# An AdaLN block with an H3 attention and a mixture of experts: spectral units spread over two batch rows, the barrier ahead of the heads left out, and three smaller reorderings

## The chip, the cores and the metric

The kernel runs on one core of a Trainium2 chip. The metric is the device time of one execution in microseconds (us); the times shown are those of the runs named below. Engines: TensorE (PE in the rows; PEld its weight load), VectorE (DVE), ScalarE (ACT), GpSimd (POOL) and SyncE (SP), which issues most DMAs.

## The reference

Four batch rows of 1024 tokens with 256 features, 32 bit. Two modulated layer norms enclose an H3 attention and a top-2 mixture of eight experts:

```python
mod = (silu(c) @ wmod).reshape(4, 6, 1, 256)
sa, ca, ga, sb, cb, gb = ...
h = layernorm(x) * (1 + ca) + sa
x = x + ga * h3_attention(h)
h = layernorm(x) * (1 + cb) + sb
x = x + gb * moe(h)

def h3_attention(u):
    q, k, v = (u @ W.T + b for each of three)
    k = causal_conv(k, ssm_k_kernel) + ssm_k_D * k
    kv = k[:, :, i] * v[:, :, j]
    y = causal_conv(kv, ssm_kernel) + D * kv
    return (q * y).sum(over i) @ Wo.T + bo
```

Heads are groups of 8 features (32 of them), so each head convolves 64 products. The taps are 512 long in both convolutions. The experts take at most 1280 tokens each.

## The kernel before

Everything lives in SBUF: `qkv` holds q, v and k of all 32 tiles of 128 tokens, and a large `arena` is cut into regions by hand, so who may write where is a matter of order. Each engine has its own program, written out in order, and waits on semaphores; there is no scheduler.

**Rows.** For each batch row `b`, TensorE turns the normalised row (`h_transposes`, L1325), VectorE modulates the turned pieces (`h_rows`, L860, four a row), ScalarE and GpSimd split them into a high and a low part, and TensorE makes eight tiles of q, v and k (`qkv_products`, L1344), twelve matmuls each. Two pairs of PSUM banks take the tiles in turn, and tile t waits until VectorE has added the bias to tile t - 2 (`qkv_rows`, L900).

**Units.** The convolution of k goes through a spectrum. A unit is half the columns of one batch row, eight in all. For each unit TensorE runs `forward` (L1365, 16 matmuls of 256 columns, f32), ScalarE copies four banks (`spec_out`, L683), VectorE joins the parities, turns a half, multiplies by the spectrum of the taps and folds (`joined_spectrum` to `folded_product`, L368 to L415), TensorE runs `inverse` (L1379), and ScalarE copies the result into `k_stage` (`conv_out`, L691). There are two buffers of spectra and two of folded products. `forward(0)` stands after the third row, `forward(1)` in the middle of the fourth, and after that inverses alternate with forwards three ahead. VectorE makes units 0 and 1 between the bias adds of the fourth row, beginning after the third.

**Turning K.** From `k_stage` SyncE sends k back into the token layout in `qkv`, one batch row (two units) at a time, four DMAs of 256 KB each (L473 to L478). Both engines that reuse `k_stage` or read k wait for `k_turned`.

**Barrier.** After this stage every engine drains and waits for all five (`stage_end`, L337). SyncE loads the first two Toeplitz blocks of the heads just ahead of it:

```python
            sp.wait_ge(fold_ready[1], UNITS)
            load_toeplitz(0)
            load_toeplitz(1)
            sp.wait_ge(k_turned, 64 * (B + 1))
            stage_end(sp, 1)
```

**Heads.** For each of 32 heads VectorE multiplies k and v (`products`, L1001, four quarters), ScalarE and GpSimd split products and Toeplitz block (L705 on, L569 to L578), TensorE multiplies (L1436), and VectorE gates and sums.

**Behind the heads.** For each row: `y_transposes`, `attention_out`, then `residual` and statistics on VectorE, `normalize` on ScalarE (L725, eight tiles, one signal), `h2_transposes` (L1468, four groups in two banks), copies with the modulation (`h2_turned`, L734), `router` (L1481), logits and choice on VectorE. After that come a threshold search and the experts.

At the start TensorE runs five matmuls on zeros (L1288), the modulation, the first transposes, and then waits for the split of the first row.

## Time and profile before

| | us |
|---|---|
| median of 3 runs | 1224.91 (1223.55 to 1226.75) |
| profiled execution, its own time | 1222.99 |
| span of its profile | 1221.2 |
| TensorE busy | 1123.6 (92% of the span) |
| VectorE busy | 820.2 (67%) |
| ScalarE busy | 420.5 (34%) |
| GpSimd busy | 546.0 (45%) |

The profile is of one execution; its span begins and ends a little inside the time that is measured. Times in the rows are microseconds from the start of the span. Of the chain of work that ended last, the page puts 83% on TensorE, 7% on VectorE and 2% each on ScalarE, DMA, GpSimd and time without a visible wait. A busy share says little by itself here: the stages have different limits, so the stretch around the change has to be read by itself. By stretches, the rows of the batch and the units lie from 17 to 233 us, the heads from 244 to about 580, the routing to about 660, and the rest is the threshold search and the experts.

### The profile page before, as it was taken

Reading aid. Unit: us, or ns where it says so; the run is one execution under the profiler, and the core shown is the slowest. Engines: PE = TensorE matmul, PEld = TensorE weight load, DVE = VectorE, ACT = ScalarE, POOL = GpSimd, SP = SyncE. Lnnn points to the kernel's source line nnn. Section 1 sums busy time; section 2 is a strip of 40 time slices with the busy share of each in tenths; the row PEclk is TensorE's granted clock in tenths of the full one; section 3 lists DMA queues with packets and bytes.
Section 4 is the critical chain, followed back from the end, with each engine's and each line's share of the span. In section 5 each row is a group of like instructions: output and inputs, shape, how many; then the busy total and the mean of one; then the engine's idle time right before and its main releaser. Section 6 shows DMA issues by size and latency. Waiting matters only on the chain.

```text
span 1221.2 us, 16986 instructions
## 1 busy us (share of the span) xinstructions
PE 1123.6 (92%) x5754; PEld 974.4 (80%) x5754; DVE 820.2 (67%) x1549; ACT 420.5 (34%) x762; POOL 546.0 (45%) x403
## 2 busy tenths in 40 slices
PE   7999999499999999999985548999999999999996
PEld 5878888388888888887775447889898989899996
DVE  5576999579999999999576785454444444444442
ACT  5321222223333333331562212343443534344432
POOL 3130000177777777774000022566565656565723
PEclk8999999799999999999985557999999999999998
DMA  7100022343111011002440212754544443534322
GB/s 263 35 35 1 1 52 50 104 142 102 32 32 32 32 32 32 32 21 69 139 144 7 100 56 68 192 146 68 134 91 117 83 121 79 132 73 78 60 42 27
DMA packets 69633, 93.35 MB, mean 76 GB/s; under 512 B 5668, under 2 KB 57636, under 8 KB 69592
## 3 DMA queue, kind: packets, MB, share of 16 engines
q1 hardware_dynamic: 51576, 60.96, 15.9%
q0 software_dynamic: 18016, 31.86, 13.6%
q8 instruction: 24, 0.39, 0.1%
q14 instruction: 17, 0.14, 0.0%
HBM read 65.29 MB, written 23.31 MB: 73 GB/s over the span
## 4 chain that ended last, share of the span: by engine, by line
PE 83%; DVE 7%; issue 2%; ACT 2%; DMA 2%; POOL 2%; SPq 0%; DVEq 0%; POOLq 0%; ACTq 0%
PE ps L1436 27%; PE ps L1575 18%; PE ps L1591 12%; PE ps L1592 6%; PE ps L1386 5%; PE ps L1375 4%; PE ps L1356 4%; PE ps L1464 2%; DVE arena L1141 1%; PE ps L1557 1%; PE ps L1485 1%; DVE qkv L819 1%; DMA qkv<-in_w 1%; PE ps L1537 1%; DVE arena_rounded L819 1%
## 5 line engine op out<-in xcount | busy, mean ns | idle before, releaser
L1575 PE MATMUL ps<-arena_rounded,w_high 128*128 128x384 f32 (+1 forms) x768 | 211.4, 356 | 2.1 <-DVE arena_rounded L819 2.1
L578 POOL TENSOR_TENSOR kv_low<-arena,kv_high 128x512 fp32r<-128x512 f32 x128 | 187.1, 1491 | 38.7 <-ACT kv_high L630 38.7
L1436 PE MATMUL ps<-kv_high,toep_high 128*128 128x512 f32 (+1 forms) x512 | 193.9, 379 | 11.1 <-POOL kv_low L578 11.1
L1436 PE MATMUL ps<-kv_low,toep_high 128*128 128x512 f32 (+1 forms) x512 | 193.9, 379 | 0.0
L1436 PE MATMUL ps<-kv_high,toep_low 128*128 128x512 f32 (+1 forms) x512 | 193.0, 377 | 0.0
L1258 DVE SCALAR_TENSOR_TENSOR hidden_low<-ps,hidden_high 128x384 fp32r<-128x384 f32 (+1 forms) x192 | 115.6, 602 | 100.1 <-ACT hidden_high L788 99.7
L602 POOL DMA_INDIRECT out<-arena x80 | 126.2, 1578 | 105.1 <-DVE arena L819 97.4
L591 POOL DMA_INDIRECT qkv<-row_scratch,arena x80 | 82.6, 1033 | 185.3 <-DVE arena L1212 159.2
L1575 PEld LDWEIGHTS ps<-arena_rounded,w_high 128*128 128x128 f32 x768 | 140.4, 190 | 13.4 <-issue 2.5
L819 DVE TENSOR_TENSOR arena<-qkv 128x512 f32 (+1 forms) x128 | 136.8, 1127 | 12.5 <-SPq L339 12.5
L788 ACT ACTIVATE hidden_high<-ps 128x384 fp32r<-128x384 f32 (+1 forms) x192 | 101.3, 528 | 126.7 <-PE ps L1575 126.7
L573 POOL TENSOR_TENSOR toep_low<-arena,toep_high 128x640 fp32r<-128x640 f32 x32 | 50.1, 1566 | 198.4 <-ACT toep_high L630 198.4
L1575 PE MATMUL ps<-arena_rounded,w_low 128*128 128x384 f32 (+1 forms) x384 | 136.5, 355 | 0.0
L1268 DVE SCALAR_TENSOR_TENSOR arena<-ps,qkv,arena 128x256 f32<-128x256 f32 x80 | 38.7, 484 | 139.1 <-ACT arena L803 139.1
L1436 PEld LDWEIGHTS ps<-kv_high,toep_high 128*128 128x128 f32 x512 | 96.9, 189 | 29.9 <-POOL kv_low L578 11.5
L1591 PE MATMUL ps<-arena_rounded,hidden_high 128*128 128x512 f32 x320 | 113.1, 397 | 3.2 <-DVE arena L1268 3.2
L1591 PE MATMUL ps<-qkv_rounded,hidden_high 128*128 128x512 f32 x320 | 113.6, 398 | 0.0
L630 ACT ACTIVATE kv_high<-arena 128x512 fp32r<-128x512 f32 x128 | 78.7, 632 | 100.1 <-DVE arena L819 100.1
L1436 PEld LDWEIGHTS ps<-kv_high,toep_low 128*128 128x128 f32 x512 | 96.7, 189 | 18.0
L1436 PEld LDWEIGHTS ps<-kv_low,toep_high 128*128 128x128 f32 x512 | 97.0, 189 | 17.7
L1019 DVE TENSOR_REDUCE qkv<-arena 128x512 f32 (+1 forms) x128 | 87.8, 686 | 18.9 <-DVE arena L819 4.7
L819 DVE TENSOR_TENSOR arena<-ps,qkv 128x512 f32<-128x512 f32 x128 | 87.4, 683 | 13.5 <-PE ps L1436 13.4
(194 smaller groups left out, 1954.2 us busy)
## 6 DMA issues: line engine op xcount, KB each, us to landing
arena<-ssm_scratch SPq DMA_DIRECT2D x32, 320.0 KB, 3.2
qkv<-in_w SPq DMA_DIRECT2D x16, 512.0 KB, 5.1
qkv<-in_w SPq DMA_DIRECT2D x8, 1024.0 KB, 8.8
arena<-in_u SPq DMA_DIRECT2D x7, 1024.0 KB, 6.2
row_scratch<-qkv SPq DMA_DIRECT2D x4, 1056.0 KB, 4.6
qkv<-arena SPq DMA_DIRECT2D x16, 256.0 KB, 3.4
row_scratch<-arena SPq DMA_DIRECT2D x4, 1024.0 KB, 6.4
out<-qkv SPq DMA_DIRECT2D x4, 1024.0 KB, 9.3
```

The costliest lines, as they stand in the source:

```text
L578: nc.gpsimd.tensor_tensor(kv_parts[s][1][:, quarter], kv_flat[s][:, quarter], kv_parts[s][0][:, quarter].bitcast(F32), ALU.subtract).then_ ...
L591: nc.gpsimd.indirect_dma_start(qkv[:, 16 + j, D:WIDE], None, row_dram[:, :], bass.IndirectOffsetOnAxis(ap=from_row[:, column:column + 1], ...
L602: nc.gpsimd.indirect_dma_start(out[:, :], bass.IndirectOffsetOnAxis(ap=to_row[:, column:column + 1], axis=0), y_sb[column % RING], None, c ...
L630: return nc.scalar.activation(dst, src, ACT.Copy)
L788: nc.scalar.activation(hid_parts[0][:, BANK * f:BANK * f + width], ps[:, f % 4, 0:width], ACT.Relu).then_inc(hid_high, 1)
L819: return nc.vector.tensor_tensor(o, a, b_, op)
L1019: nc.vector.tensor_reduce(qkv[:, tiles, bass.ds(h * NJ, NJ)], qy[g], AX.X, ALU.add).then_inc(head_summed, 1)
L1258: nc.vector.scalar_tensor_tensor(hid_parts[1][:, BANK * f:BANK * f + width], ps[:, f % 4, 0:width], 0.0, hid_parts[0][:, BANK * f:BANK * f ...
L1436: last = mm(ps[:, 4 * s + g, (lo - 2 * g) * B * 64:BANK], toep_parts[s][a][:, o * P:(o + 1) * P], kv_parts[s][x][:, src], start=n == 0 and ...
L1575: last = mm(ps[:, f % 4, 0:width], w1_parts[q][a][:, dc * F + f * P:dc * F + (f + 1) * P], xeT_parts[x][dc][:, 0:width], start=dc == 0 and ...
L1591: mm(ps[:, bank].rearrange("p (a d) -> p a d", a=2), high, w2_parts[q][:, :, f], start=f == 0, stop=False)
L1592: last = mm(ps[:, bank, 0:D], low, w2_parts[q][:, 0, f], start=False, stop=f == FC - 1)
```

## The change

- **Units.** `forward(0)` moves into the third row, after its sixth tile, `forward(1)` behind that row's last tile, `forward(2)` into the middle of the fourth row and `forward(3)` behind it; inverses then alternate with forwards four ahead. VectorE joins unit 0 ahead of the third row's last bias add, makes the rest of unit 0 before the fourth row's adds, and units 1 and 2 between them, four adds each. The second `clamp` of the modulation moves from tile 6 to tile 3 of the third row.
- **Buffers.** There are three folded buffers (unit 1 has a place of its own), and unit 0 has its own spectrum buffer.
- **Turning K.** SyncE turns K by unit, with DMAs of 128 KB (rows of 512 bytes), one semaphore for each parity of the unit.
- **Barrier.** It is left out. The Toeplitz block of head 0 is loaded ahead of the first turn, that of head 1 after unit 2, both to other places. VectorE makes the products of heads 0 and 1 by batch row, three rows as soon as they are turned, the last when its two units are.
- **Filler.** Four matmuls of 512 columns follow the first transposes; 24 matmuls of 128 columns follow the last inverse.
- **Router.** `normalize` signals after four tiles and after eight; transposes go by half row, and the router starts on a half.

The core of the diff; buffer addresses and declarations are left out:

```diff
+FILL_FIRST, FILL_HEADS = 4, 24
...
+        def spectrum_of(unit):
+            return parity_spec[0 if unit == 0 else 1 + unit % 2]
+        def folded_of(unit, parity):
+            return (folded_1 if unit == 1 else folded[unit % 3])[parity]
...
         def folded_product(dve, link, unit):
-            if unit >= 2:
-                dve.wait_ge(conv_psum, CT * (unit - 1))
+            if unit >= 3:
+                dve.wait_ge(conv_psum, CT * (unit - 2))
...
-            with sp.Fori(0, B) as b:
-                for parity in range(2):
-                    sp.wait_ge(conv_ready, 2 * CT * b + 2 * CT + (parity + 1) * CT // 2)
-                    for half in range(2):
-                        dst = tile_view[parity::2, half::2, bass.ds(b, 1), 2 * D:3 * D].rearrange("p t o n -> p t (o n)")
-                        sp.dma_start(dst, k_stage[half * P // 2:(half + 1) * P // 2, parity::2]).then_inc(k_turned, 16)
...
-            sp.wait_ge(fold_ready[1], UNITS)
             load_toeplitz(0)
-            load_toeplitz(1)
-            sp.wait_ge(k_turned, 64 * (B + 1))
-            stage_end(sp, 1)
+            for unit in range(UNITS):
+                e = slice(2 * D + columns(unit).start, 2 * D + columns(unit).stop)
+                for parity in range(2):
+                    sp.wait_ge(conv_ready, CT * unit + CT + (parity + 1) * CT // 2)
+                    for half in range(2):
+                        sp.dma_start(tile_view[parity::2, half::2, unit // 2, e],
+                                     k_stage[half * P // 2:(half + 1) * P // 2, parity::2, columns(unit)]).then_inc(k_turned[unit % 2], 16)
+                if unit == 2:
+                    load_toeplitz(1)
+            for i in range(2):
+                sp.wait_ge(k_turned[i], 64 * B)
...
-                    if i == 0 and unit % 2 == 0:
-                        act.wait_ge(k_turned, 32 * unit + 64)
+                    if i == 0 and unit >= 2:
+                        act.wait_ge(k_turned[unit % 2], 64 * (unit // 2))
...
-                last.then_inc(norm2_ready, 1)
+                    last.then_inc(norm2_ready, 1)
...
-                    if b == 2 and t == 6:
+                    if b == 2 and t == 3:
                         clamp(GB - 2)
+                    if b == 2 and t == TB - 1:
+                        dve.wait_ge(consts_in, 16 * 8)
+                        joined_spectrum(dve, link, 0)
...
+            for unit, t in ((1, 0), (2, TB // 2)):
+                qkv_rows(B - 1, t)
+                joined_spectrum(dve, link, unit)
+                qkv_rows(B - 1, t + 1)
+                turned_half(link)
+                qkv_rows(B - 1, t + 2)
+                real_products(link, unit)
+                qkv_rows(B - 1, t + 3)
...
-            stage_end(dve, 1)
...
-            products(0, 0)
-            products(1, 1)
+            for b in range(B - 1):
+                for i in range(2):
+                    dve.wait_ge(k_turned[i], 64 * (b + 1))
+                for h in range(2):
+                    first_products(h, b)
+            for i in range(2):
+                dve.wait_ge(k_turned[i], 64 * B)
+            for h in range(2):
+                first_products(h, B - 1).then_inc(kv_ready, 4)
...
+            for _ in range(FILL_FIRST):
+                mm(ps[:, 7, :], idle[:, 0:P], idle, start=True, stop=True)
...
+                if b == B - 2:
+                    qkv_products(b, range(TB // 2, TB - 2))
+                    forward(0)
+                    qkv_products(b, range(TB - 2, TB))
+                    forward(1)
+                    continue
                 if b == B - 1:
-                    forward(1)
+                    forward(2)
                 qkv_products(b, range(TB // 2, TB))
...
-                if b == B - 2:
-                    forward(0)
-            forward(2)
+            forward(3)
...
                 inverse(unit)
-                if unit + 3 < UNITS:
-                    forward(unit + 3)
-            stage_end(pe, 1)
+                if unit + 4 < UNITS:
+                    forward(unit + 4)
+            pe.wait_ge(spec_ready, JP * UNITS + 4)
+            pe.wait_ge(consts_in, 16 * 8)
+            for _ in range(FILL_HEADS):
+                mm(ps[:, 0, 0:P], group_ones[:], ident[:], start=True, stop=True)
...
                 for g in range(4):
+                    half, dc = g // 2, g % 2
+                    if dc == 0:
+                        pe.wait_ge(norm2_ready, 2 * b + half + 1)
...
-                pe.wait_ge(h2T_ready, 4 * b + 4)
                 for tb in range(TB):
+                    if tb % 4 == 0:
+                        pe.wait_ge(h2T_ready, 4 * b + tb // 2 + 2)
```

VectorE, from the end of the third row, before. The line L819 on 128x768 is a bias add, L363 and L364 the join, L377 and L378 the turned half, L387 and L388 the real products:

```order
L819 TENSOR_TENSOR qkv<-ps,arena 128x768 x3
L363 TENSOR_TENSOR arena<-arena 128x512
L364 TENSOR_TENSOR arena<-arena 128x512
L363 TENSOR_TENSOR arena<-arena 128x512
L364 TENSOR_TENSOR arena<-arena 128x512
L819 TENSOR_TENSOR qkv<-ps,arena 128x768
L377 SCALAR_TENSOR_TENSOR arena<-arena,sign_sb 128x4x128
L378 SCALAR_TENSOR_TENSOR arena<-arena,sign_sb 128x4x128
L819 TENSOR_TENSOR qkv<-ps,arena 128x768
L387 TENSOR_TENSOR arena<-arena 128x1024
```

The same place of the change; its lines are L821 for the add, L368 and L369 for the join, L382 and L383 for the turned half, L392 to L407 for products, difference and sum, L418 for the fold:

```order
L368 TENSOR_TENSOR arena<-arena 128x512
L369 TENSOR_TENSOR arena<-arena 128x512
L821 TENSOR_TENSOR qkv<-ps,arena 128x768
L382 SCALAR_TENSOR_TENSOR arena<-arena,sign_sb 128x4x128
L383 SCALAR_TENSOR_TENSOR arena<-arena,sign_sb 128x4x128
L392 TENSOR_TENSOR arena<-arena 128x1024
L393 TENSOR_TENSOR arena<-arena 128x1024
L397 TENSOR_TENSOR arena<-arena 128x1024
L402 TENSOR_TENSOR arena<-arena 128x1024
L403 TENSOR_TENSOR arena<-arena 128x1024
L407 TENSOR_TENSOR arena<-arena 128x1024
L418 TENSOR_TENSOR arena<-arena 128x512 x4
```

Before, an add of the fourth row stands between every two steps of unit 0. In the change the add in this piece is the third row's last, and the rest of unit 0 runs to its fold without an add.

TensorE, from the last forwards to the first head, before. L1375 is a forward, L1386 an inverse, L1436 a head:

```order
L1375 MATMUL ps<-qkv,arena 128x256 x16
L1386 MATMUL ps<-arena 128x256 x16
L1375 MATMUL ps<-qkv,arena 128x256 x16
L1386 MATMUL ps<-arena 128x256 x48
L1420 UNCONDITIONAL_BRANCH
L1420 ISA
L1425 ISA
L1436 MATMUL ps<-kv_high,toep_high 128x512
```

And in the change, where L1391 is a forward, L1402 an inverse, L1440 the filler and L1459 a head:

```order
L1391 MATMUL ps<-qkv,arena 128x256 x16
L1402 MATMUL ps<-arena 128x256 x16
L1391 MATMUL ps<-qkv,arena 128x256 x16
L1402 MATMUL ps<-arena 128x256 x64
L1440 MATMUL ps<-ident_sb,group_ones_sb 128x128 x24
L1443 UNCONDITIONAL_BRANCH
L1443 ISA
L1448 ISA
L1459 MATMUL ps<-kv_high,toep_high 128x512
```

Four inverses, not three, stand behind the last forward, and 24 filler matmuls behind them.

## Rows read from the trace of the kernel before

**Rows 1.** Chain of work in order of time: start us, us, what

```profile
74.34 8.58 PE ps L1356 x48
...
133.90 6.91 PE ps L1386 x32
...
216.81 7.15 issue
223.96 8.99 PE ps L1386 x32
232.98 0.39 ACT arena L630
...
234.22 3.52 DMA qkv<-arena
...
242.26 1.73 POOL kv_low L578
```

**Rows 2.** Windows: stretch, us, each engine's busy time, granted TensorE clock, DMA share, GB/s

```profile
17.00:22.80 5.80, 5.80 (x21) 5.22 (x22) 2.88 (x7) 0.68 (x2) 0.46 (x1) 0.50 0.90 306
216.90:220.80 3.90, 0.00 (x0) 0.00 (x0) 3.83 (x4) 0.33 (x1) 0.00 (x0) 1.00 0.00 0
221.00:227.60 6.60, 3.64 (x9) 2.95 (x10) 4.03 (x6) 0.00 (x0) 0.00 (x0) 0.50 0.00 0
244.00:248.00 4.00, 3.98 (x11) 3.30 (x12) 3.59 (x4) 1.26 (x2) 4.00 (x3) 0.50 0.83 328
```

**Rows 3.** Timeline of VectorE: start us, us, engine, line, operation, tiles, count

```profile
88.03 0.81 DVE L867 TENSOR_SCALAR arena<-ps,modT 128x512 f32<-128x512 f32 x1 [0.44 <-POOL hT_low L561]
...
90.49 0.53 DVE L873 TENSOR_SCALAR arena<-arena 4x256 f32<-4x256 f32 x1
...
92.67 0.96 DVE L819 TENSOR_TENSOR qkv<-ps,arena 128x768 f32<-128x768 f32 x1
...
121.50 1.82 DVE L819 TENSOR_TENSOR qkv<-ps,arena 128x768 f32<-128x768 f32 x2 [0.15 <-DVE arena L413]
...
139.26 0.69 DVE L363 TENSOR_TENSOR arena<-arena 128x512 f32<-128x512 f32 x1 [0.15 <-DVE arena L413]
...
141.91 0.75 DVE L377 SCALAR_TENSOR_TENSOR arena<-arena,sign_sb 128x512 f32<-128x512 f32 x1
...
211.11 0.69 DVE L363 TENSOR_TENSOR arena<-arena 128x512 f32<-128x512 f32 x1 [0.15 <-DVE arena L413]
...
237.80 8.42 DVE L819 TENSOR_TENSOR arena<-qkv 128x512 f32<-128x512 f32 x8 [12.55 <-SPq L339]
```

**Rows 4.** Page, costliest groups: ScalarE's split of products, busy and mean ns, idle before

```profile
L630 ACT ACTIVATE kv_high<-arena 128x512 fp32r<-128x512 f32 x128 | 78.7, 632 | 100.1 <-DVE arena L819 100.1
```

**Rows 5.** Source view of L478, the sixteen DMAs that turn K

```profile
DMA to landing us min/median/max: 3.2/3.4/3.6
```

**Rows 6.** Timeline of TensorE at the start

```profile
1.47 6.70 PE L1288 MATMUL ps<-arena 128*128 128x512 f32 x10 [1.47 <-DVE arena L930]
...
16.92 0.76 PE L1356 MATMUL ps<-wqkv_high,hT_high 128*128 128x512 f32 x1 [4.70 <-POOL hT_low L561]
...
22.45 0.67 PE L1356 MATMUL ps<-wqkv_high,hT_high 128*128 128x512 f32 x1
```

**Rows 7.** Timeline of all engines, router of the first and the last row

```profile
596.49 1.10 PE L1477 MATMUL ps<-ident_sb,qkv 128*128 128x128 f32 x8 [0.52 <-ACT qkv L730]
...
637.85 4.04 ACT L730 ACTIVATE qkv<-qkv,shift,std 128x256 f32<-128x256 f32 x8 [0.47 <-DVE shift L1060]
...
641.94 3.95 PE L1477 MATMUL ps<-ident_sb,qkv 128*128 128x128 f32 x16 [2.37 <-ACT qkv L730]
...
645.08 1.63 ACT L738 ACTIVATE arena<-ps,modT 128x512 f32<-128x512 f32 x2 [0.35 <-PE ps L1477]
...
646.76 6.99 PE L1485 MATMUL ps<-wr_sb,arena 128*128 128x8 f32 x32 [0.87 <-ACT arena L738]
...
653.79 0.23 DVE L1073 COPY arena<-ps 128x64 f32<-128x64 f32 x1 [0.86 <-PE ps L1485]
```

More of the change, by code:

```diff
@@ L185, in adaln_block @@
         kv_parts = [parts(f"kv{i}", FT + 4096 * i, [P, 2048]) for i in range(2)]
-        toep_raw = [region(WQ0 + TOEP * i, TOEP) for i in range(2)]
+        toep_raw = [region(start, TOEP) for start in (KK0 + 3328, MA0 + 2 * TOEP)]
         toep_parts = [parts(f"toep{i}", start, [P, TOEP]) for i, start in enumerate((KK0, MA0))]
@@ L269, in adaln_block @@
         row_dram = nc.dram_tensor("row_scratch", [TOKENS, ROW], F32)
-        stage_done = [sem(f"stage{k}_done") for k in range(8)]
         chain_v, chain_g = sem("vector_chain"), sem("gpsimd_chain")
@@ L412, in folded_product @@
                     j = part * JP // 2
-                    last = nc.vector.tensor_tensor(folded[unit % 2][parity][:, j:j + JP // 2], v[:, 0:JP // 2], v[:, JP // 2:JP], op)
+                    last = nc.vector.tensor_tensor(folded_of(unit, parity)[:, j:j + JP // 2], v[:, 0:JP // 2], v[:, JP // 2:JP], op)
                 link(last)
@@ L687, in spec_out @@
                     act.wait_ge(spec_psum, JP * unit + j + 1)
-                    copy(parity_spec[unit % 2][:, 2 * j:2 * j + 2],
+                    copy(spectrum_of(unit)[:, 2 * j:2 * j + 2],
                          ps[:, j].rearrange("p (o h e) -> p o h e", o=2, h=2)).then_inc(spec_ready, 1)
@@ L693, in conv_out @@
                     act.wait_ge(conv_psum, CT * unit + i + 1)
-                    if i == 0 and unit % 2 == 0:
-                        act.wait_ge(k_turned, 32 * unit + 64)
+                    if i == 0 and unit >= 2:
+                        act.wait_ge(k_turned[unit % 2], 64 * (unit // 2))
                     copy(k_stage[:, c::CT, columns(unit)],
                          ps[:, 4 + c, 0:D].rearrange("p (h e) -> p h e", h=2)).then_inc(conv_ready, 1)
-            for unit in range(3):
+            for unit in range(4):
                 spec_out(unit)
@@ L702, in _ @@
                 conv_out(unit)
[L703 to L705 removed]
+                if unit + 4 < UNITS:
+                    spec_out(unit + 4)
             with act.Fori(0, HEADS // 2) as hh:
@@ L978, in _ @@
             folded_product(dve, link, 0)
-            qkv_rows(B - 1, 4)
-            qkv_rows(B - 1, 5)
-            joined_spectrum(dve, link, 1)
-            qkv_rows(B - 1, 6)
-            turned_half(link)
-            qkv_rows(B - 1, 7)
-            real_products(link, 1)
-            real_difference(link)
-            imaginary_products(link, 1)
-            imaginary_sum(link)
-            folded_product(dve, link, 1)
-            for unit in range(2, UNITS):
+            for unit, t in ((1, 0), (2, TB // 2)):
[6 more added lines that the diff above has]
+                qkv_rows(B - 1, t + 3)
+                real_difference(link)
+                imaginary_products(link, unit)
+                imaginary_sum(link)
+                if unit == 1:
+                    dve.wait_ge(hT_low, 4 * B)
+                    dve.wait_ge(mod_out, 16)
+                folded_product(dve, link, unit)
+            for unit in range(3, UNITS):
                 joined_spectrum(dve, link, unit)
@@ L1386, in inverse @@
                         last = mm(ps[:, 4 + c, 0:D].rearrange("p (h e) -> p h e", h=2), idft[:, j, c * P:(c + 1) * P],
-                                  folded[unit % 2][c % 2][:, j], start=j == 0, stop=j == JP - 1)
+                                  folded_of(unit, c % 2)[:, j], start=j == 0, stop=j == JP - 1)
                     last.then_inc(conv_psum, 1)
```

50 lines of the change are left out of this document (21 added, 29 removed).

## The prediction

> **What bounds the kernel now.** I read the page's chain first: TensorE carries most of it, so what counts is where TensorE waits or runs at its low clock. The chain in order of time then shows one large hole around the change [rows 1]. The seventh inverse ends at 216.81, TensorE stands 7.15 us until VectorE has folded unit 7, the last inverse takes 8.99 instead of 6.91 us, and from its end at 232.95 another 11.1 us pass before the first head multiplies at 244.0: a copy, a DMA of 3.52 us, products, splitting on ScalarE and GpSimd. The table of windows gives the clock beside it [rows 2]: 1.2 GHz (0.50) from 221.0 to 227.6 and again for the first 4 us of the heads; earlier also from 17.0 to 22.8, after an idle of 4.70 us [rows 6]. In the idle of 7.15 us the clock was still up after 4.0 us and down by 4.2. VectorE's timeline [rows 3] says why the hole exists: five units take 71.85 us from 139.26 to 211.11, 14.37 each, while TensorE needs 2 x 6.91 = 13.82 a unit, so VectorE is behind when the last unit comes.
>
> **1. Units inside the third and fourth rows.** VectorE's work stays the same and starts sooner, but its bias adds, which free TensorE's banks, now stand behind unit work. I walk both queues with: a tile 8.58/4 = 2.15 us, a forward or inverse 6.91 [rows 1]; a bias add 0.86 to the next instruction and 0.96 to its end, a join 141.91 - 139.26 = 2.65, the other steps of a unit 11.72 [rows 3].
> The second clamp, 92.67 - 90.49 = 2.18 us, moves ahead of the last row's four transposed pieces. The last of these started at 88.03 and took 0.81 [rows 3]; now it ends at 91.0. Forward 0 needs it. TensorE's first four tiles of row three end at 82.92 [rows 1], its transposes and two more tiles at 88.9, so it idles 2.2 us. Forward 0 runs to 98.0, tiles 6 and 7 to 102.3, forward 1 to 109.2, tiles 0 and 1 of the last row to 113.5. VectorE meanwhile: add 6 at 100.2, join 0 to 103.7, add 7 to 104.6, rest of unit 0 to 116.3, add 0 done at 117.3. Tile 2 waits for that add: **idle 3.8 us**. Tile 3 waits for the next add, behind join 1, until 120.8 (1.3 us); forward 2 ends at 129.9, tiles 4 and 5 at 134.2. Unit 1 with its four adds ends at 116.3 + 14.37 + 3.4 = 134.1, so tile 6 starts at 135.1 (0.9 us) and tile 7 at 138.6 (1.4 us). Forward 3 ends at 147.7; twelve forwards and inverses without a gap follow, 82.9 us, to 230.6. VectorE ends unit 2 at 152.0 and five more at 223.8; the last inverse begins at 223.7 and needs only the first of the fold's two halves. So TensorE becomes the bound, with about 1 us to spare: the 7.15 us and the low clock of the last inverse go, and 9.6 us of smaller idles take their place. Against 232.95 that is 2.3 us; the restarts after five idles are not in the walk, so I take **2.0** (0.5 to 2.5). With the third folded buffer each inverse that VectorE asks for has ended over 8 us before.
>
> **2. The gap ahead of the heads.** The barrier itself cost nothing: the DMA landed at 237.74 and VectorE started at 237.80 [rows 1, 3]. What shrinks is the work. From the end of the last inverse: copy 0.42, two DMA issues 0.85, landing, one product 8.42/8 = 1.05 [rows 3], ScalarE's split 0.63 [rows 4], GpSimd's 1.73 [rows 1], 0.2 of handovers. The Toeplitz block, which GpSimd split first, is now loaded early and split while the DMA flies. Three quarters of the products are made beside the last inverse (six of 1.05 us after 223.8, done at 230.1). For the landing of half the bytes the nearest row is the sixteen DMAs of now, 3.2 to 3.6 us [rows 5]; below that nothing in the rows excludes 2.3. I take 3.2, since the smaller size was never seen. Sum 8.1 against 11.1: **3.0** (2.6 to 3.9).
> The Trainium skill ("DMA: Bandwidth & Descriptors", Anatomy of one DMA) gives a fixed cost of about 2.0 us and the bytes over 436 GB/s; by that, an estimate, 128 KB land in 2.3 us and the gain would be 3.9. It is fitted for GpSimd's queue, and no run here shows this size.
>
> **3. Filler matmuls ahead of the heads.** 24 matmuls of 128 columns, f32. An inverse makes 32 records of 256 columns in 6.91 us, 0.216 each [rows 1]; 48 records of half the columns take 48 x 0.108 = 5.2 us. They stand in the 8.1 us gap and leave an idle of 2.9, less than the 4.0 after which the clock was still up [rows 2]. So the heads start at 2.4 GHz. Before, 4.0 us ran at half [rows 2], worth 2.0. At full clock the first quarter (2304 columns) takes 1.0 us and GpSimd's next split 1.73 [rows 1], so 0.7 comes back as a wait: **1.3** (0 to 2.0). From there the heads are one stretch of TensorE, so all of this reaches the end.
>
> **4. Filler at the start.** Four matmuls of 512 columns between 12.2 and 16.92. Five of the same took 6.70 us [rows 6], 1.34 each: 5.4 us, to 17.6, where the first tile is ready at 16.92. That tile and eight transposes took until 22.45 at 1.2 GHz, 5.5 us; at 2.4 GHz they take 2.15 + 0.9. The second tile then starts at 20.7 instead of 22.45, and its own first record was slow too (0.67). VectorE's add of that tile stands ahead of row two's statistics, and those ahead of the transposes that TensorE waits for next, so it is handed on: **2.0**. If the clock never falls, 2.6; if the filler is slow throughout (to 19.0) and the clock rises no sooner than now, a loss of 2.0.
>
> **5. Half-row router.** A row's first transposes need only four of eight scaled tiles. In the first row TensorE waited 0.52 us for the eighth [rows 7]; that and a copy brought forward give 0.6. In the last row ScalarE scales from 637.85 (4.04 us), TensorE waits until 641.94, the last copy ends at 646.71, and the router takes 6.99 at the low clock [rows 7]. Now the first two groups are turned from 639.9; groups three and four follow at 642.8 and 643.9, each once a copy (0.82) has freed its bank; the router starts on its first half at 644.9 and ends at 651.9 instead of 653.75. VectorE reaches that logit copy (653.79 now) at 652.0, since the exponential ahead of it comes 1 us sooner. 1.8 + 0.6 = **2.4** (1.0 to 3.0).
>
> **Sum.** 2.0 + 3.0 + 1.3 + 2.0 + 2.4 = 10.7 us. The profiled execution took 1222.99 us (span 1221.2): 1212.3. The median of the runs shown is 1.9 above it, so **1214.2**.
>
> **Rivals.**
> *The clock falls in the new idle of 3.8 us.* It held for 4.0 and was down by 4.2 [rows 2], so it is close. The price is that of the last inverse, 8.99 - 6.91 = 2.1 [rows 1], on a TensorE that is now the bound: 1216.3. Chance 0.17. The Trainium skill ("TensorE: Matmul & The Clock Gate", HAM oscillation) names just such gaps between matmuls as what throttles the engine again; by that rule this is the case that comes.
> *The filler at the start does nothing or costs.* It begins where the clock is about to fall. 2.0 to 4.0 lost: 1216.2 to 1218.2, say 1217. Chance 0.13.
> *Hardly any gain.* Both of these, and the heads begin at the low clock as well: 10.7 - 2.1 - 4.0 - 1.3 = 3.3, or 1221.6. Here the edits do not do what they say. Chance 0.06.
> *Slower: the clock stays low through the fourth row.* After the idle of 3.8 us come three of 0.9 to 1.4 within 25 us. If these keep it at 1.2 GHz until 140.8, six tiles and forward 2, 19.8 us of work, take twice as long; the idles absorb 3.6, and 16.2 goes through: 1230.4. It decides from about 18 us of such work on (10.7 + 3.7 + 3.6). Against it: after 7.15 us of idle the clock was back within 4 us of work [rows 1, 2]. Chance 0.03.
> *More than forecast.* Landing at 2.3, clock held at the start: 1212.7 or a little below. Chance 0.06.
>
> **How the numbers follow.** The forecast has 0.55. The range takes in the better case, the first two rivals and a little of their overlap: 1209.5 to 1219.5. Within 0.3% (3.7 us) is about what a measurement of this kernel cannot tell from no change; above 1221.2 lie only part of the third rival and the fourth. Faster 0.89, the same 0.07, slower 0.04.
>
> **What would show it.** No idle before the last inverse, which takes 6.9 us and ends near 228.6 (230.6 less the 2.0 of the start); idles of about 2 and 4 us in the third and fourth rows; a first head some 8 us after the last inverse, at 2.4 GHz from its first matmul; a last router that ends 2.4 us sooner after the heads. Wrong would be an idle before the last inverse (VectorE still bounds), or a granted clock of 0.50 behind the 3.8 us idle or at the first head.

## The result and the profile after

The changed kernel takes **1212.36 us**, median of four runs (1209.35 to 1213.68), beside 1225.83 for the kernel before in the same comparison: a ratio of 0.9888 with a 95% interval of 0.9876 to 0.9899, so 12.4 to 15.2 us less. One of the kernel before's four executions there took 1316.28 us, in a slower state of the chip; it is in that median (1224.91 without it) and not in the ratio. The profiled execution took 1209.35 us (span 1207.5), the lowest of the four; the one before took 1222.99. The span's 13.7 us, cut at five points that both traces have (TensorE's times):

| stretch | before | after | gain |
|---|---|---|---|
| start to the end of the last inverse | 232.94 | 228.79 | 4.15 |
| from there to the first head | 11.09 | 6.34 | 4.75 |
| first head to the first matmul behind the heads (`y_transposes`) | 330.97 | 329.29 | 1.68 |
| from there to the first matmul of the threshold search | 84.53 | 83.39 | 1.14 |
| from there to the end of the span | 561.67 | 559.69 | 1.98 |

In the tables below the third stretch is called the heads, the fourth the routers and the fifth the rest. The change does not touch the rest.

TensorE at the start, from the four filler matmuls on, two records each (they answer to [rows 6]). Columns are start, duration, engine, line, operation, tiles, shape, count, idle before and what ended it:

```profile
13.43 4.67 PE L1379 MATMUL ps<-arena 128*128 128x512 f32 x8
...
20.82 0.48 PE L1370 MATMUL ps<-wqkv_high,hT_high 128*128 128x512 f32 x1
```

The second tile starts 1.63 us sooner, although the weights of the modulation came 0.76 us later here (9.55 instead of 8.79 for the first matmul on them).

TensorE from the third row to the heads:

```profile
89.08 7.14 PE L1391 MATMUL ps<-qkv,arena 128*128 128x256 f32 x32 [1.97 <-issue]
...
115.38 0.80 PE L1370 MATMUL ps<-wqkv_high,hT_high 128*128 128x512 f32 x1 [3.87 <-DVE qkv L821]
...
136.63 0.50 PE L1370 MATMUL ps<-wqkv_high,hT_high 128*128 128x512 f32 x1 [0.85 <-DVE qkv L821]
...
213.73 15.06 PE L1402 MATMUL ps<-arena 128*128 128x256 f32 x69
228.62 5.52 PE L1440 MATMUL ps<-ident_sb,group_ones_sb 128*128 128x128 f32 x48
235.13 0.50 PE L1459 MATMUL ps<-kv_high,toep_high 128*128 128x512 f32 x1 [0.99 <-POOL kv_low L580]
```

Of the idle of 7.15 us and the slow last inverse [rows 1] nothing is left: the inverses run without a gap. In their place stand 1.97, 3.87 and 0.85 us. The windows answer to [rows 2] (granted clock third from the end):

```profile
115.40:122.00 6.60, 6.60 (x21) 5.55 (x22) 6.42 (x9) 0.00 (x0) 0.00 (x0) 0.55 0.00 0
129.20:135.70 6.50, 6.50 (x38) 5.59 (x36) 6.03 (x10) 0.60 (x1) 0.00 (x0) 1.00 0.00 0
235.00:241.00 6.00, 5.87 (x28) 4.84 (x29) 2.76 (x4) 3.00 (x6) 6.00 (x6) 1.00 0.86 303
```

The granted clock did fall at the end of the idle of 3.87 us (the window from 115.4 has 0.55), and the two tiles behind it ran at 1.2 GHz. It was back at 1.00 for the next tiles, and the heads start at 2.4 GHz. The gap ahead of the heads, on VectorE, ScalarE and GpSimd:

```profile
221.68 3.70 DVE L821 TENSOR_TENSOR arena<-qkv 128x512 f32<-128x512 f32 x6 [0.22 <-DVE arena L418]
232.38 1.29 DVE L821 TENSOR_TENSOR arena<-qkv 128x512 f32<-128x512 f32 x2 [6.99 <-DMA qkv<-arena]
...
228.82 0.38 ACT L632 ACTIVATE arena<-ps 128x256 f32<-128x256 f32 x1 [1.34 <-PE ps L1402]
...
233.10 2.19 ACT L632 ACTIVATE kv_high<-arena 128x512 fp32r<-128x512 f32 x4 [3.27 <-DVE arena L821]
...
229.91 1.54 POOL L575 TENSOR_TENSOR toep_low<-arena,toep_high 128x640 fp32r<-128x640 f32 x1 [138.92 <-ACT toep_high L632]
233.81 5.02 POOL L580 TENSOR_TENSOR kv_low<-arena,kv_high 128x512 fp32r<-128x512 f32 x4 [2.36 <-ACT kv_high L632]
```

GpSimd now splits the Toeplitz block while the DMA flies. In the kernel before, ScalarE could split that block only from 239.50 on, when its load had landed, 1.8 us behind K. And of the eight products of then [rows 3] the first five took 3.10 us and the last three, beside GpSimd's splits, 5.41:

```profile
239.50 0.74 ACT L630 ACTIVATE toep_high<-arena 128x640 fp32r<-128x640 f32 x1 [6.14 <-DMA arena<-ssm_scratch]
...
237.80 3.10 DVE L819 TENSOR_TENSOR arena<-qkv 128x512 f32<-128x512 f32 x5 [12.55 <-SPq L339]
240.81 5.41 DVE L819 TENSOR_TENSOR arena<-qkv 128x512 f32<-128x512 f32 x3
```

So a product by itself took 0.62 to 0.65 us in both kernels, and 1.05 was a mean of two kinds. GpSimd's four splits take 5.02 now, 1.26 each. The DMAs of half the size land faster than the old ones [rows 5]:

```profile
DMA to landing us min/median/max: 2.4/2.4/3.2
```

The last router, ScalarE, TensorE and VectorE (they answer to [rows 7]):

```profile
628.33 4.04 ACT L732 ACTIVATE qkv<-qkv,shift,std 128x256 f32<-128x256 f32 x8 [0.47 <-DVE shift L1074]
...
630.45 1.97 PE L1501 MATMUL ps<-ident_sb,qkv 128*128 128x128 f32 x8 [1.51 <-ACT qkv L732]
634.91 6.83 PE L1510 MATMUL ps<-wr_sb,arena 128*128 128x8 f32 x32
...
642.07 0.22 DVE L1087 COPY arena<-ps 128x64 f32<-128x64 f32 x1
```

From the first scaling to VectorE's copy of the logits it takes 13.74 us instead of 15.94.

### The profile page after: what moved, and what is told of

Read it like the earlier page. It is cut to its first block, busy times and chain, and to the rows that moved or that the text cites. A ratio compares the mean times of both kernels' runs of the same rounds, so it can differ in the third digit from the quotient of the medians.

```text
span 1207.5 us, 17088 instructions
## 1 busy us (share of the span) xinstructions
PE 1129.0 (93%) x5810; PEld 980.5 (81%) x5810; DVE 816.3 (68%) x1549; ACT 420.4 (35%) x762; POOL 544.8 (45%) x403
## 4 chain that ended last, share of the span: by engine, by line
PE 73%; issue 13%; DVE 7%; ACT 2%; DMA 2%; POOL 2%; SPq 0%; DVEq 0%; POOLq 0%; ACTq 0%
PE ps L1459 27%; PE ps L1600 18%; PE ps L1616 12%; PE ps L1617 6%; PE ps L1487 2%; PE ps L1370 2%; DVE arena L1155 1%; PE ps L1582 1%; DMA qkv<-in_w 1%; DVE qkv L821 1%; PE ps L1562 1%; DVE arena_rounded L821 1%; PE ps L1545 1%; PE ps L1510 1%; ACT qkv L732 1%
## 5 line engine op out<-in xcount | busy, mean ns | idle before, releaser
L1459 PE MATMUL ps<-kv_high,toep_high 128*128 128x512 f32 (+1 forms) x512 | 193.1, 377 | 1.0 <-POOL kv_low L580 1.0
L1459 PE MATMUL ps<-kv_low,toep_high 128*128 128x512 f32 (+1 forms) x512 | 193.1, 377 | 0.0
L1459 PE MATMUL ps<-kv_high,toep_low 128*128 128x512 f32 (+1 forms) x512 | 192.4, 376 | 0.0
L821 DVE TENSOR_TENSOR arena<-qkv 128x512 f32 (+1 forms) x128 | 133.3, 1099 | 7.2 <-DMA qkv<-arena 7.0
L1459 PEld LDWEIGHTS ps<-kv_high,toep_high 128*128 128x128 f32 x512 | 96.4, 188 | 19.7 <-POOL kv_low L580 1.2
L1459 PEld LDWEIGHTS ps<-kv_high,toep_low 128*128 128x128 f32 x512 | 96.1, 188 | 18.0
L1459 PEld LDWEIGHTS ps<-kv_low,toep_high 128*128 128x128 f32 x512 | 96.4, 188 | 17.4
L821 DVE TENSOR_TENSOR arena<-ps,qkv 128x512 f32<-128x512 f32 x128 | 87.4, 683 | 15.5 <-PE ps L1459 15.4
```

The costliest lines, as they stand in the source:

```text
L821: return nc.vector.tensor_tensor(o, a, b_, op)
L1459: last = mm(ps[:, 4 * s + g, (lo - 2 * g) * B * 64:BANK], toep_parts[s][a][:, o * P:(o + 1) * P], kv_parts[s][x][:, src], start=n == 0 and ...
```

## The experiments

Each is the changed kernel with one edit, or with one set of edits where the text says so. In the expectations "mine" is the author's account and "rival" another one. "Median" is that of its runs; the kernel before had medians of 1226.5 to 1227.5 beside them, so one comparison may lie about a microsecond off another. The columns after it are the stretches of the table above, from each one's profiled execution.

| run | median | end of last inverse | gap | heads | routers | rest |
|---|---|---|---|---|---|---|
| changed, again | 1211.33 | 229.36 | 6.40 | 329.30 | 83.37 | 559.9 |
| no filler at the start | 1212.80 | 232.17 | 6.41 | 329.29 | 83.38 | 560.2 |
| no filler ahead of the heads | 1215.17 | 228.82 | 6.36 | 330.45 | 85.03 | 562.6 |
| whole-row router | 1215.97 | 229.45 | 6.33 | 329.27 | 84.57 | 563.1 |
| barrier | 1217.28 | 229.98 | 9.46 | 330.65 | 83.66 | 560.3 |
| two folded buffers | 1219.29 | 235.39 | 6.34 | 329.29 | 83.60 | 563.2 |
| late clamps | 1209.63 | 226.94 | 6.35 | 329.29 | 83.39 | 562.5 |
| filler in the fourth row | 1214.15 | 230.18 | 6.35 | 329.31 | 83.38 | 563.6 |
| adds inside the units | 1214.38 | 231.45 | 6.36 | 329.27 | 83.38 | 562.3 |
| early forward | 1208.59 | 226.50 | 6.36 | 329.28 | 83.38 | 560.6 |
| the same, filler ahead of the last inverse | 1209.87 | 224.59 | 6.40 | 329.28 | 85.02 | 563.7 |
| the same, VectorE's order changed | 1214.40 | 228.44 | 7.53 | 330.88 | 83.41 | 562.4 |

The rest is the same program in all, and yet takes 560 to 564 us. Most of this goes with the clock. In the first group of experts TensorE waits 1.8 us for VectorE, and behind that wait the clock held in one execution (first fence: changed, again) and fell in another (second: late clamps). Windows, with the granted clock third from the end:

```profile
748.50:752.50 4.00, 2.31 (x13) 2.04 (x14) 2.88 (x5) 0.42 (x1) 1.02 (x1) 1.00 0.00 0
752.50:756.50 4.00, 4.00 (x27) 3.53 (x26) 0.91 (x2) 0.83 (x2) 3.39 (x3) 1.00 0.55 62
```

```profile
746.50:750.50 4.00, 2.29 (x9) 1.96 (x10) 2.90 (x5) 0.45 (x1) 1.00 (x1) 0.79 0.00 0
750.50:754.50 4.00, 4.00 (x20) 3.43 (x20) 0.91 (x2) 0.47 (x1) 2.18 (x2) 0.78 0.57 60
```

So a difference of 2 to 3 us between medians of four to six runs can come from there, and each experiment below is judged first in the stretch that it edits.

**The changed kernel again.**

> The changed kernel again, unaltered, as the baseline of the experiments. Every theory: 1212 us, within 1.5 us (its four earlier executions lay between 1209.35 and 1213.68).

1211.33 (1209.97 to 1212.65), as expected, in two pairs 2.5 us apart (1209.97 and 1210.12, 1212.54 and 1212.65).

**No filler at the start.**

```diff
-FILL_FIRST, FILL_HEADS = 4, 24
+FILL_FIRST, FILL_HEADS = 0, 24
```

> Without the four products that TensorE computes for nothing ahead of the first tile (the other 24 stay). Mine: the first two tiles run at 1.2 GHz again, the second one starts at about 22.4 us instead of 20.8, and the kernel takes 2 us longer, about 1214. Rival: VectorE, which adds the tiles, or the turned input of the next row, sets that stretch, and the time stays at 1212.

1.5 us longer by the medians, which alone would not tell mine from the rival. The first fence is this run, the second the changed kernel again:

```profile
16.95 0.76 PE L1370 MATMUL ps<-wqkv_high,hT_high 128*128 128x512 f32 x1 [4.68 <-POOL hT_low L566]
...
90.74 8.83 PE L1391 MATMUL ps<-qkv,arena 128*128 128x256 f32 x32 [1.99 <-issue]
```

```profile
29.29 3.16 PE L1354 MATMUL ps<-ident_sb,arena 128*128 128x128 f32 x16 [2.25 <-ACT arena L644]
...
89.63 7.14 PE L1391 MATMUL ps<-qkv,arena 128*128 128x256 f32 x32 [1.98 <-issue]
```

The idle of 4.68 us is back and the second tile starts at 22.48 instead of 20.50: 2.0 us, as mine said. But the changed kernel had lost part of it again by 29.29: its clock fell in the next idle of 2.25 us and sixteen transposes took 3.16 us, where those after a slow start took 1.97. The end of the first row's last tile, counted from the first matmul on the modulation's weights, is 33.57 us here, 32.10 in the changed kernel again and 31.17 in its first profile, where the clock held. So the filler is worth 1.5 to 2.4 us. The other 1.7 us by which the last inverse is later here is the first forward at the low clock (8.83 us beside 7.14), after an idle that is the same in both.

**No filler ahead of the heads.**

```diff
-FILL_FIRST, FILL_HEADS = 4, 24
+FILL_FIRST, FILL_HEADS = 4, 0
```

> Without the 24 products for nothing between the last inverse and the first head. Mine: TensorE idles some 6.5 us there, the first 4 us of the heads run at 1.2 GHz as in the kernel before, and the kernel takes 1.3 to 2 us longer, 1213.3 to 1214. Rival: GpSimd's splits bound the first head anyway, and the time stays at 1212. The start of the first head, 6.5 us behind the last inverse, is the same by both.

```profile
235.10:239.00 3.90, 3.82 (x12) 3.20 (x13) 1.23 (x2) 2.95 (x6) 3.90 (x5) 0.61 0.97 298
```

The window of the first 3.9 us of heads has the low clock (1.00 in the changed kernel). The start of the first head does not move (6.36 us), and the heads take 1.15 us more. That is just below the 1.3 to 2 of mine; the rival, under which nothing would have changed, is out. The medians' 3.8 us hold more than that: in the profile another 1.7 in the routers and 2.8 in the rest, where the clock was low for longer. Whether those two follow from the missing filler stays open.

**Whole-row router.**

```diff
-                    half, dc = g // 2, g % 2
-                    if dc == 0:
-                        pe.wait_ge(norm2_ready, 2 * b + half + 1)
+                    half, dc = g % 2, g // 2
+                    if g == 0:
+                        pe.wait_ge(norm2_ready, 2 * b + 2)
```

(with one signal of 2 after all eight tiles, and the products behind all four groups)

> The router by whole rows again (one signal after all eight tiles, the transposes in the old order, the products wait for all four groups), all else as changed. Mine: the last row's router, from the first scaling to the copy of the logits, takes 2.2 us longer (15.9 instead of 13.7), and the kernel 2.4 us, about 1214.4. Rival: what decides in that stage is how often the granted clock falls to 0.50 there, and with fewer idle stretches it falls once less, so the time is 1211 to 1213.

TensorE and VectorE in the last router:

```profile
632.00 3.95 PE L1501 MATMUL ps<-ident_sb,qkv 128*128 128x128 f32 x16 [2.39 <-ACT qkv L732]
636.83 7.00 PE L1509 MATMUL ps<-wr_sb,arena 128*128 128x8 f32 x32 [0.87 <-ACT arena L740]
...
643.86 0.22 DVE L1087 COPY arena<-ps 128x64 f32<-128x64 f32 x1 [0.85 <-PE ps L1509]
```

Scaling began at 627.91, so this router took 15.95 us: 2.2 more, as mine said. But counted from the end of the heads it began 1.06 us sooner, because the clock held in the first router. Its products, first in this run, then in the changed kernel again:

```profile
591.74 3.64 PE L1509 MATMUL ps<-wr_sb,arena 128*128 128x8 f32 x32
```

```profile
591.06 4.99 PE L1510 MATMUL ps<-wr_sb,arena 128*128 128x8 f32 x32
```

The next attention output took 7.15 us here and 9.12 there. Halving the row gains 2.2 and gives 1.1 back through one more stretch at 1.2 GHz, so in the routers' stretch it is worth 1.2. The rival's mechanism, one fall of the clock less, was there too, but smaller than what mine gained. The medians' 4.6 us have 3.2 of the rest in them.

**Barrier.**

```diff
+        def stage_end(eng, k):
+            eng.drain().then_inc(stage_done[k], 1)
+            eng.wait_ge(stage_done[k], 5)
...
+            stage_end(act, 1)
             with act.Fori(0, HEADS // 2) as hh:
```

(and so on the other four engines; on TensorE behind its filler)

> The barrier of all five engines ahead of the heads put back, all else as changed (VectorE still makes the first three rows' products before it, TensorE stands behind its filler). Mine: what the barrier cost was the Toeplitz split behind the landing of K, so the first head starts about 1 us later, 7.5 us behind the last inverse instead of 6.5, and the kernel takes 1 us longer, 1213. Rival: the barrier itself cost the 4.6 us by which that gap shrank, and the time is 1216 or more.

ScalarE and VectorE in the gap:

```profile
235.65 0.74 ACT L640 ACTIVATE toep_high<-arena 128x640 fp32r<-128x640 f32 x1 [5.25 <-PEq L342]
...
235.46 1.29 DVE L830 TENSOR_TENSOR arena<-qkv 128x512 f32<-128x512 f32 x2 [8.90 <-PEq L342]
```

By its time, 1217.28, the run is the rival's; by its rows it is neither's. The gap is 3.1 us longer where mine has 1 and the rival 4.6. The engine that arrived last at the barrier was TensorE's queue (PEq), behind the filler: my edit made the filler part of the wait. Without it K would have let VectorE start near 233.6 (an estimate: the last copy ended at 230.39, and in the changed kernel again VectorE starts 3.23 us behind that copy). So about 1.8 us is the filler, and the 1.2 left is the Toeplitz split behind the barrier, close to mine. The heads then started on a lower clock, which cost 1.35 us, and the rest of the 6 us lies in other stretches. The run shows that the split was on the path and that a barrier makes any filler ahead of it a price; it does not show the barrier alone.

**Two folded buffers.**

```diff
-            if unit >= 3:
-                dve.wait_ge(conv_psum, CT * (unit - 2))
+            if unit >= 2:
+                dve.wait_ge(conv_psum, CT * (unit - 1))
```

> Each fold waits for the inverse before last's successor, as with two folded buffers: a fold of unit n waits until the inverse of unit n-2 has read its buffer; all else as changed. Mine: the fold of unit 2 waits for the first inverse (to about 153 us), VectorE falls some 6 us behind and TensorE waits for it ahead of the later inverses, 4 to 6 us in all: 1216 to 1218. Rival: there is slack between the folds and the inverses, and the time stays at 1212.

VectorE, then TensorE:

```profile
153.71 2.73 DVE L418 TENSOR_TENSOR arena<-arena 128x512 f32<-128x512 f32 x4 [6.00 <-PE ps L1402]
...
226.56 8.83 PE L1402 MATMUL ps<-arena 128*128 128x256 f32 x32 [3.88 <-issue]
```

The fold of unit 2 waits 6.00 us for the first inverse, VectorE never makes it up, TensorE idles 3.88 us ahead of the last inverse and runs it at the low clock: the last inverse ends 6.0 us later, as mine said; the median lies above mine's 1218, with 3.3 us more in the rest. The last inverse ends at 235.39, later than the 232.94 of the kernel before: without the third buffer the units moved forward gain nothing.

**Late clamps.**

```diff
-                    if b == 2 and t == 2:
-                        clamp(GA - 2)
-                    if b == 2 and t == 3:
-                        clamp(GB - 2)
+                    if b == 2 and t == 6:
+                        clamp(GA - 2)
+                        clamp(GB - 2)
```

> VectorE's two clamps in the third row moved from between the adds of tiles 2 and 4 to behind the add of tile 5, where VectorE idles 7.6 us. Mine: the idle of 2.0 us ahead of the first forward goes, all that follows comes 2 us sooner, and the time is 1210. Rival: TensorE stands 2 us earlier ahead of the next tile of the last row and waits there instead, so the time stays at 1212.

```profile
87.14 7.14 PE L1390 MATMUL ps<-qkv,arena 128*128 128x256 f32 x32
```

The idle ahead of the first forward is gone. From the end of the first row's last tile to the end of the last inverse it takes 186.2 us instead of 188.1, so 1.8 of the 2.4 us by which the last inverse ends sooner are the edit's and the others come from the start. The median is 1.7 us lower. As mine said.

**Filler in the fourth row.** Fourteen products for nothing between tiles 1 and 2 of the last row:

```diff
+                    qkv_products(b, range(2))
+                    pe.wait_ge(spec_ready, JP * 3)
+                    pe.wait_ge(consts_in, 16 * 8)
+                    for _ in range(FILL_ROW):
+                        mm(ps[:, 0, 0:P], group_ones[:], ident[:], start=True, stop=True)
+                    qkv_products(b, range(2, TB // 2))
```

> Fourteen products for nothing (3.2 us at 2.4 GHz) in the idle of 3.9 us ahead of the third tile of the last row, after which the granted clock fell to 0.50. Mine: the third and fourth tile take 4.5 us instead of 7.2, but TensorE then waits for VectorE's adds ahead of later tiles by as much, and the time stays at 1212. Rival: the slow clock cost what the two tiles show, and the time is 1209.5.

```profile
112.74 3.29 PE L1419 MATMUL ps<-ident_sb,group_ones_sb 128*128 128x128 f32 x28
116.86 0.47 PE L1370 MATMUL ps<-wqkv_high,hT_high 128*128 128x512 f32 x1 [0.83 <-DVE qkv L821]
120.27 0.50 PE L1370 MATMUL ps<-wqkv_high,hT_high 128*128 128x512 f32 x1 [1.07 <-DVE qkv L821]
...
134.50 0.50 PE L1370 MATMUL ps<-wqkv_high,hT_high 128*128 128x512 f32 x1 [0.76 <-DVE qkv L821]
138.02 0.50 PE L1370 MATMUL ps<-wqkv_high,hT_high 128*128 128x512 f32 x1 [1.14 <-DVE qkv L821]
```

The clock stays up and each of four tiles now waits for an add of VectorE's, where the slow tiles waited once, 0.85. No time is won and none lost: from the end of the first forward to the start of the fourth it takes 42.6 us, as in the changed kernel. The last inverse ends 0.8 us later because the first forward, ahead of the edit, had the low clock in this execution (8.83 us instead of 7.14); the median is 2.8 higher, with 3.7 of the rest. The other runs say the same: in all nine profiles with this order of the fourth row that stretch took 42.6 to 42.7 us, whether the clock was low for two tiles, for about one or for none. The low clock in the fourth row costs nothing, because VectorE's adds set the pace there. As mine said.

**Adds inside the units.** The last row's add 0 ahead of unit 0's sum, adds 1 to 4 in unit 1, 5 to 7 in unit 2 (the second unit's part of the edit):

```diff
-            for unit, t in ((1, 0), (2, TB // 2)):
+            for unit, t in ((1, 1), (2, 5)):
...
-                qkv_rows(B - 1, t + 3)
                 real_difference(link)
                 imaginary_products(link, unit)
+                if unit == 1:
+                    qkv_rows(B - 1, 4)
```

> The last row's adds of tiles moved forward among the units' work on VectorE: the add of tile 0 before unit 0's sum, tiles 1 to 4 inside unit 1, tiles 5 to 7 inside unit 2; no work added or removed. Mine: the idle of 3.9 us ahead of the third tile shrinks, but VectorE is only 1 to 1.7 us ahead of TensorE at the end of the last inverses and sets the end then: the time is 1210.5. Rival: TensorE alone bounds, and the time is 1208.5.

```profile
118.80 0.79 PE L1372 MATMUL ps<-wqkv_high,hT_high 128*128 128x512 f32 x1 [2.63 <-DVE qkv L821]
...
137.69 0.50 PE L1372 MATMUL ps<-wqkv_high,hT_high 128*128 128x512 f32 x1 [1.92 <-DVE qkv L821]
```

A miss for both. The wait of 3.87 became one of 2.63 a tile later (add 1 now stands behind unit 0's fold), and the wait of 0.85 ahead of the last tile became 1.92 (add 5 stands behind unit 1's fold): 4.55 us instead of 4.72. What the order won, 0.75 us to the start of the fourth forward, that forward lost again at the low clock behind the second wait (7.92 us instead of 7.07). The last inverse ends 2.1 us later, 1.7 of it from the first forward, which had the low clock in this execution.

**Early forward.** The first forward ahead of the last row's transposes, the clamps and the first join later, the adds spread over units 0 to 2:

```diff
+                if b == B - 2:
+                    pe.wait_ge(modT_ready, 4)
+                    pe.wait_ge(mod_read, 1)
+                    forward(0)
                 if b + 1 < B:
                     h_transposes(b + 1)
```

> A version meant to beat both: the first forward runs ahead of the last row's transposes, in TensorE's wait for VectorE; the clamps stand behind the add of tile 4 and the first join behind that of tile 6; the last row's adds 0 and 1 stand in unit 0, 2 to 5 in unit 1, 6 and 7 in unit 2. Mine: both idles (2.0 and 3.9 us) go, VectorE is ahead by as much since it starts unit 0 sooner, and the time is 1208, between 1207 and 1209. Rival: VectorE sets the end of the inverses, and the time is 1210.5 to 1212.

```profile
217.05 9.46 PE L1407 MATMUL ps<-arena 128*128 128x256 f32 x32 [4.72 <-issue]
```

1208.59, the time of mine, but with the rival's mechanism. Both idles went; then TensorE comes 10 us sooner to its fourth forward (129.29 instead of 139.41), and from there VectorE, which needs 14.28 us a unit where TensorE needs 13.81, sets the end again; the idle and the low clock ahead of the last inverse are back.

**The same with filler ahead of the last inverse.**

```diff
+                if unit == UNITS - 1:
+                    pe.wait_ge(spec_ready, JP * UNITS + 4)
+                    pe.wait_ge(consts_in, 16 * 8)
+                    for _ in range(FILL_LAST):
+                        mm(ps[:, 0, 0:P], group_ones[:], ident[:], start=True, stop=True)
                 inverse(unit)
```

> The version with the early forward, and in its idle of 4.7 us ahead of the last inverse 20 products for nothing (4.6 us at 2.4 GHz). Mine: the last inverse still waits for VectorE's last fold but takes 7.1 us instead of 9.5, so it ends 2.4 us sooner, near 224.1, and the kernel takes 1206.2 us. Rival: VectorE's fold sets the pace of the inverse's pieces too, and the time stays at 1208.6.

```profile
212.56 4.63 PE L1445 MATMUL ps<-ident_sb,group_ones_sb 128*128 128x128 f32 x40
217.45 7.14 PE L1407 MATMUL ps<-arena 128*128 128x256 f32 x32 [0.27 <-issue]
```

In its stretch mine holds: the last inverse takes 7.14 us and ends at 224.59 (expected 224.1). The median, 1209.87, misses the 1206.2 and does not show the gain; beside the run before, the profiled execution has 1.6 us more in the routers and 3.1 in the rest, where the clock was low for longer. Its lowest run, 1207.47, is the lowest of all.

**The same with VectorE's order changed** (six products for nothing; the part that decided):

```diff
+                        h_rows(b + 1, (0, 1))
+                        dve.wait_ge(consts_in, 16 * 8)
+                        joined_spectrum(dve, link, 0)
+                        h_rows(b + 1, (2, 3))
```

> As the run before, with six products for nothing instead of 20, and VectorE's order changed where it idled: the first join between the second and third turned pieces of the fourth row, the adds of tiles 6 and 7 of the third row inside unit 0, the last row's adds 0 and 1 behind unit 0's fold, and 2 to 7 inside units 1 and 2. Mine: VectorE, which bounds the eight units at 14.3 us each, loses 2.5 us of idle time, TensorE waits some 2 us ahead of the last inverse, which ends near 221.7, and the kernel takes 1204 us. Rival: TensorE now stands waiting for the later adds and becomes the bound, and the time is 1206 or more.

VectorE, GpSimd, TensorE:

```profile
90.69 0.68 DVE L368 TENSOR_TENSOR arena<-arena 128x512 f32<-128x512 f32 x1
91.29 1.78 DVE L369 TENSOR_TENSOR arena<-arena 128x512 f32<-128x512 f32 x1
93.00 1.77 DVE L368 TENSOR_TENSOR arena<-arena 128x512 f32<-128x512 f32 x1
...
90.80 3.42 POOL L566 TENSOR_TENSOR hT_low<-arena,hT_high 128x512 fp32r<-128x512 f32 x2 [26.13 <-ACT hT_high L632]
...
98.04 0.79 PE L1381 MATMUL ps<-wqkv_high,hT_high 128*128 128x512 f32 x1 [3.37 <-DVE qkv L821]
```

A miss, 1214.40. The joins that were to fill VectorE's idle fell beside GpSimd's splits: two of the four took 1.78 us instead of 0.68, the third and fourth turned pieces and the adds behind them came late, and TensorE waited 3.37 us. It waited another 2.45 us ahead of the first inverse, and the gap and the heads were longer too (7.53 and 330.88 us).

**What is left.** Late clamps, the early forward and the early forward with filler have the lowest ratios to the kernel before (0.9859, 0.9863, 0.9859) and end the last inverse 2.4 to 4.8 us sooner than the changed kernel again. By the whole time none of the three is set apart from the changed kernel again, which has a ratio of 0.9874 (0.9858 to 0.9891).

## Why the prediction was right

1212.4 came where 1214.2 was forecast, within the range. That it came so close is partly luck: in the profiled execution the gap gave 1.75 us more than forecast and the routers 1.26 less, the rest gave 1.98 that no term holds, and that execution lies 3.0 us below the median of its four, where the forecast had counted 1.9.

**Units inside the rows (2.0) and the filler at the start (2.0).** Together 4.15 in the first profile. Cut at the end of the first row's last tile (42.52 before, 40.72 after), 1.80 of it is the start, although the modulation's weights came 0.76 later, and 2.35 the units. The walk of both queues held: idles of 1.97 and 3.87 us where 2.2 and 3.8 were worked out, the last inverse's end at 228.79 where 228.6 was, VectorE's last fold done at 221.46, just ahead of the last inverse at 221.7. What failed inside it: of the waits of 1.3, 0.9 and 1.4 us in the fourth row only one of 0.85 came. The low clock had taken their place. By the run without it the filler at the start is worth 1.5 to 2.4, depending on the clock in the next idle.

**The first rival's condition came and its price did not.** The clock fell behind 3.87 us of idle, as the rival said, which the prediction had also named as a sign of being wrong; two tiles took 7.20 instead of 4.48 us; and the time did not move. The rival counted those 2.1 us on "a TensorE that is now the bound", but in the fourth row each tile waits for an add of VectorE's, and the filler there showed that fast tiles only wait longer. The rule of the Trainium skill ("TensorE: Matmul & The Clock Gate", HAM oscillation) that such gaps throttle the engine agrees with the 0.55 of that window; it says nothing of whether the stretch is on the path.

**The gap ahead of the heads (3.0).** Measured 4.75, outside the 2.6 to 3.9 given for it; the first head came 6.3 us behind the last inverse, not 8. The step was right in kind and short in three terms: the landing took 2.4 us instead of 3.2, a product 0.65 instead of 1.05, GpSimd's split 1.26 instead of 1.73. The rows taken for them were of other conditions. The landing was of DMAs of 256 KB. The product was a mean of eight, of which only the last three met GpSimd's splits; the one on the path, the first, had taken about 0.65 before as well. The split was one beside those products (in the change only two products are left, and they end before GpSimd's split begins). By the rows, 1.26 us of the 4.75 lie ahead of VectorE's first product (mostly the smaller DMA), 3.03 between that product and GpSimd's split (the Toeplitz block, whose load and splitting had stood there) and 0.45 behind. No run puts back the larger DMA or the late load alone, so these three shares are read and not tested. The Trainium skill ("DMA: Bandwidth & Descriptors", Anatomy of one DMA) gave 2.3 us for the landing as an estimate; the trace's 2.4 agrees, on SyncE's queue. By the same formula 256 KB would take 2.6 us, an estimate; there the trace has 3.4 [rows 5]. That the barrier cost nothing in itself is not shown: the run that put it back measured the filler ahead of it too.

**The filler ahead of the heads (1.3).** Heads 1.68 shorter; without it 1.15 longer. Of the wait of 0.7 for GpSimd 0.1 came back, since its splits were faster.

**The half-row router (2.4).** The last router gained 2.2 (1.8 forecast), but the routers' stretch 1.14. The missing microsecond went to the clock, which in the changed kernel fell in the first router too, where the whole-row one kept it.

**The rest.** 2.0 us less in the profiled execution and not in the sum. It is no part of the change: the rest takes 559.7 to 563.7 over the fourteen profiled executions. Between these two, 1.1 us come from the clock in the first group of experts, which rose 87.0 us into the stretch before and 84.6 us into it in the change, and about 0.5 from a wait for VectorE behind that group's start; why the clock rose sooner no run shows.

## What to carry over

When two engines alternate on shared buffers, walk both queues before pricing a slow clock or a wait: in the fourth row a low clock on TensorE was free, since the other engine's adds set the pace, while the same low clock on the last inverse cost its full 2 us. Moving one engine's work forward pays only up to the next buffer: without the third folded buffer 6.0 us were lost again. And take durations for a step from rows in which the same neighbours are at work as after the change.

## What the runs showed of the hardware that was not expected

- **The clock fell behind idles of about 2 us, in some executions.** Behind the idle of 1.97 to 1.99 us ahead of the first forward (nine profiles) the forward took 7.14 us in five and 8.83 in four. Behind the 2.25 us ahead of the second row's transposes (all fourteen profiles) these took 1.96 to 1.97 us in seven and 2.57 to 3.63 in seven. The kernel before had held its clock through 4.0 us [rows 2]. The repeated runs of one kernel lie up to 4.3 us apart; that this spread comes from such places is likely from the profiles, but each run has only one.
- **The clock fell behind idles of no more than 0.54 us** in the first router of the changed kernel again, on 32 products of 8 columns (4.99 us instead of 3.64). In the whole-row router it held behind idles of up to 0.52 us and the same products; what decides between the two is not shown.
- **VectorE and GpSimd took longer beside each other on operations with two tensors.** A VectorE join took 0.68 us alone, and two of the three that met a GpSimd split took 1.78; two of those splits took 2.54 us alone and 3.42 beside the joins. In the kernel before, the products ahead of the heads took 0.69 us alone and 1.75 to 2.03 beside GpSimd's splits, and those splits 1.73 beside the products and 1.29 behind them.
